# Gate and up weights converted from DRAM to DRAM, casts and copies moved between tiles, and the last output projections reordered

## What is computed

```python
xn = _layernorm(x)
# attention branch, H = 1024, chunk 32, 4 heads (DK 128, DV 256)
delta = shifted(xn) - xn
x5  = tanh((xn + delta * x0_mu) @ x0_w.T)            # 5 low-rank mixes
mix = einsum(x5, x2_w) + x_bias                      # r_mu, w_mu, k_mu, v_mu, g_mu
r, k, v, g = ((xn + delta * mu) @ W.T for r, k, v, g)
w   = -exp(tanh((xn + delta * w_mu) @ w_w1.T) @ w_w2.T + w_b2)
o   = chunk_rwkv6(r, k, v, w, bonus)                 # state carried over chunks
s   = (group_norm(o) * silu(g)) @ o_w.T
# feed-forward branch, int32 weights / 127, hidden size 3072
f   = (silu(xn @ wg.T) * (xn @ wu.T)) @ wd.T
out = x + s * silu(f)
```

## Time and profile before

| | |
|---|---|
| median of 3 runs | 1784.55 us |
| the profiled execution, its own time | 1784.01 us |
| its slowest core's span (core 3) | 1782.5 us |
| spans of the eight cores | 1767.7 to 1782.5 us |
| PE busy | 1674.2 us, 94% |
| DVE busy | 1089.5 us, 61% |
| ACT busy | 477.1 us, 27% |
| DMA packets of POOL's queue | 66.76 MB written, 23.8% of 16 engines |
| DMA packets of ACT's and SP's queues | 153.11 and 81.90 MB, 25.7% and 12.9% |
| casts of gate/up units | 72, median 11.2 us from issue to landing |
| loads of kept gate/up units | 120, median 3.9 us |
| keeps of gate/up units | 24, median 8.3 us |

### The profile page before, as it was taken

One profiled execution on the slowest core, in us unless ns is written; L12 is line 12 of the kernel. 1 busy time (PEld: TensorE's weight loads), 2 busy tenths in 40 slices (PEclk: granted clock), 3 DMA queues, 4 the chain that ended last, 5 costly groups with the idle time before them and its releaser, 6 DMA issues.

```text
span 1782.5 us, 26448 instructions; the slowest of 8 cores (1767.7 to 1782.5 us)
## 1 busy us (share of the span) xinstructions
PE 1674.2 (94%) x9248; PEld 779.5 (44%) x9248; DVE 1089.5 (61%) x1847; ACT 477.1 (27%) x802; POOL 164.1 (9%) x354
## 2 busy tenths in 40 slices
PE   4989939899899999999999999999999999999997
PEld 2333414344444445444544445444454445444453
DVE  5465616475765657648576567656576485764755
ACT  0133301143211432114321343114321143211411
POOL 2211300111101011000100002000010001100000
PEclk9999959999999999999999999999999999999999
DMA  8999996996669953877355344453636353464231
GB/s 160 173 168 211 214 226 157 181 181 162 195 166 221 205 188 131 257 191 226 130 176 202 130 176 168 151 188 113 210 119 225 130 176 132 138 228 142 95 109 58
DMA packets 77649, 303.46 MB, mean 170 GB/s; under 512 B 10511, under 2 KB 15056, under 8 KB 70864
## 3 DMA queue, kind: packets, MB, share of 16 engines
q10 hardware_dynamic: 31680, 153.11, 25.7%
q0 software_dynamic: 19680, 66.76, 23.8%
q1 hardware_dynamic: 26160, 81.90, 12.9%
HBM read 320.25 MB, written 44.04 MB: 204 GB/s over the span
## 4 chain that ended last, share of the span: by engine, by line
PE 80%; DMA 12%; DVE 3%; issue 2%; DVEq 1%; ACT 1%; SPq 1%; POOL 0%; ACTq 0%; POOLq 0%
PE PB L1209 16%; PE PB L1214 16%; PE PB L1334 8%; PE PB L1323 7%; PE PB L1490 6%; PE PB L1467 6%; PE PB L1362 6%; DMA sb_gu<-w_gu 4%; DMA sb_wd<-kept_wd 3%; PE PB L1429 3%; PE PB L1413 3%; DMA sb_wd<-w_fd 2%; DMA kept_gu<-sb_gu 2%; PE PB L1242 1%; DMA sb_xin<-x 1%
## 5 line engine op out<-in xcount | busy, mean ns | idle before, releaser
L1209 PE MATMUL PB<-sb_xnT,sb_gu 128*128 128x512 bf16 x1536 | 369.5, 384 | 22.2 <-DMA sb_gu<-w_gu 15.2
L1214 PE MATMUL PB<-sb_xnT,sb_gu 128*128 128x512 bf16 x1536 | 364.8, 380 | 0.0
L905 DVE SCALAR_TENSOR_TENSOR sb_xin<-PB,sb_xb,sb_dT 128x512 bf16<-128x512 f32 x320 | 218.1, 744 | 177.3 <-PE PB L1242 177.0
L686 ACT ACTIVATE sb_scr<-PB 128x512 bf16<-128x512 f32 x192 | 113.7, 597 | 576.3 <-PE PB L1214 534.5
L1209 PEld LDWEIGHTS PB<-sb_xnT,sb_gu 128*128 128x128 bf16 x1536 | 141.3, 98 | 211.9 <-issue 64.8
L1214 PEld LDWEIGHTS PB<-sb_xnT,sb_gu 128*128 128x128 bf16 x1536 | 151.0, 98 | 183.8 <-issue 4.4
L837 DVE SCALAR_TENSOR_TENSOR sb_hall<-PB,sb_scr 128x512 bf16<-128x512 f32 x192 | 130.5, 684 | 131.1 <-ACT sb_scr L686 131.1
L1323 PE MATMUL PB<-sb_wd,sb_hall 128*128 128x512 bf16 x768 | 180.1, 383 | 23.5 <-DMA sb_wd<-w_fd 21.2
L1334 PE MATMUL PB<-sb_wd,sb_hall 128*128 128x512 bf16 x768 | 179.8, 383 | 18.5 <-DMA sb_wd<-kept_wd 10.5
L695 ACT ACTIVATE sb_wc<-PB 128x512 bf16<-128x512 f32 x64 | 38.2, 597 | 326.1 <-PE PB L1334 326.1
L1334 PEld LDWEIGHTS PB<-sb_wd,sb_hall 128*128 128x128 bf16 x768 | 74.2, 98 | 109.7 <-issue 25.2
(11 more groups left out here) (149 smaller groups left out, 1705.6 us busy)
## 6 DMA issues: line engine op xcount, KB each, us to landing
sb_gu<-kept_gu ACTq DMA_DIRECT2D x120, 512.0 KB, 3.9
sb_ring<-kept_ring ACTq DMA_DIRECT2D x44, 1024.0 KB, 6.6
sb_wd<-kept_wd ACTq DMA_DIRECT2D x56, 768.0 KB, 7.5
sb_gu<-w_gu POOLq DMA_DIRECT2D x72, 512.0 KB, 11.2
sb_xin<-x SPq DMA_DIRECT2D x48, 512.0 KB, 7.6
kept_gu<-sb_gu SPq DMA_DIRECT2D x24, 512.0 KB, 8.3
sb_ring<-w_g POOLq DMA_DIRECT2D x16, 512.0 KB, 11.9
kept_ring<-sb_ring SPq DMA_DIRECT2D x8, 1024.0 KB, 15.2
```

The lines of the kernel that those rows point to most:

```text
L686: e.activation(out=sb_scr[:, p, :], in_=GB[p][:], func=AF.Silu, bias=0.0, scale=INV127).then_inc(a_silu, 1)
L905: e.scalar_tensor_tensor(out=sb_xin[:, p, c, :], in0=PM[j][:], scalar=sb_xb[:, n, c:c + 1], in1=sb_dT[:, c, :], op0=ALU.add, op1=ALU.mult) ...
L1209: e.matmul(GB[p][:], sb_gu[:, sl, 0, c, :], sb_xnT[:, c, :], start=(c == 0), stop=(c == NC - 1))
L1214: i = e.matmul(UB[p][:], sb_gu[:, sl, 1, c, :], sb_xnT[:, c, :], start=(c == 0), stop=(c == NC - 1))
```

## The change

Six things change together.

1. The gate/up units are no longer kept from SBUF. `convert(b)` issues, on POOL's queue, DMAs that read the 4-byte unit in DRAM and write bf16 to `kept_gu` in DRAM, in four batches: 6 units behind t = 2 and 4 units behind t = 3 of tile 1, 7 and 7 at the same places of tile 2. Batch 0 is cast for the last time in tile 1, the others in tile 2 (before: tiles 1, 2 and 3, eight units each). That makes 66 casts to SBUF, 24 conversions and 126 loads. `cast_gu` no longer waits for a keep, and `load_gu` waits for the whole batch of its unit.
2. The ring weights r and k are cast in tiles 0 to 2 (before 0 and 1), g in 0 to 2 (before 0 to 3), o in 0 and 1 (before 0 only). The casts of the next tile's r and k go behind t = 2 in tile 0 and behind t = 0 after it; the keeps move with them.
3. `load_wd` of the next tile's half 0 goes from the end of the tile to behind units 19 to 22 of the tile that uses it.
4. `load_res` of t = 2 and 3 waits for u = 4 of the down projection to be done, not for the last scores. In SP's order the first store goes ahead of the keeps of half 1.
5. At the start, POOL issues the first two unit casts behind the statistics of the first rows, and VectorE clears the state before any input is there.
6. In tile 7 `out_proj(2)` and the transposes for t = 3 go between the two halves of u = 7, `out_proj(2)` into other PSUM banks, and the last rows are added and stored in two halves.

The core of the diff:

```diff
-LAST_CAST_GU = [1 + (h + h // 3) % 3 for h in range(NHC)]
-LAST_CAST_RING = [1, 1, 2, 2, 3, 3, 0, 0]
+CONVERT = [[11, 13, 15, 17, 19, 21], [0, 1, 2, 3],
+           [4, 5, 6, 7, 8, 9, 10], [12, 14, 16, 18, 20, 22, 23]]
+BATCH = {hc: b for b, hcs in enumerate(CONVERT) for hc in hcs}
+LAST_CAST_GU = [1 if BATCH[h] == 0 else 2 for h in range(NHC)]
+LAST_CAST_RING = [2, 2, 2, 2, 2, 2, 1, 1]
...
+    def out_banks(it, t):
+        return PB[2:4] if it == LAST and t == 2 else P_o
...
         def load_res(it, t):
...
-                e.wait_ge(t_mt, 4 * (it + 1))
+                e.wait_ge(t_D, 8 * it + 5)
...
         def cast_gu(it, hc):
...
                 e.wait_ge(t_gu, n - NGU + 1)
-                kept = gu_counts(*divmod(n - NGU, NHC))[2]
-                if kept:
-                    e.wait_ge(k_gu[sl], 16 * kept)
...
+        def convert(b):
+            for hc in CONVERT[b]:
+                e.dma_start(kept_gu[hc], wdr["w_gu"][hc],
+                            max_dma_last_dim=8192).then_inc(k_gu[b], 16)
...
+                if t == (0 if it else 2) and nxt:
+                    for j in (0, 1):
+                        cast_ring(it + 1, j, 0)
+                        cast_ring(it + 1, j, 1)
+                if t >= 2 and it in (1, 2):
+                    convert(2 * it + t - 4)
...
         def load_gu(it, hc):
...
-            kept = gu_counts(it, hc)[2]
-            if it <= LAST_CAST + 1:
-                e.wait_ge(k_gu[sl], 16 * kept)
+            b = BATCH[hc]
+            e.wait_ge(k_gu[b], 16 * len(CONVERT[b]))
             e.dma_start(sb_gu[:, sl], kept_gu[hc]).then_inc(l_gu[sl], 16)
...
             for hc in range(19, 24):
                 silu_gu(it, hc)
+                if hc < 23:
+                    load_wd(it, 0, hc - 19)
...
                 down_first(it, 2 * t + 1)
+                if t == 3 and not nxt:
+                    out_proj(it, 2)
+                    og_transpose(it, 3)
                 down_second(it, 2 * t + 1)
```

## The result

The changed kernel took 1816.6 us, the median of four runs (1809.41 to 1818.3), beside 1786.5 (1784.49 to 1791.99) for the kernel before in the same session. The ratio is 1.0156, with a 95% interval of 1.0118 to 1.0194. The forecast was 1761, with a range that ended at 1785. The direction itself was wrong.

The account below looks back on a forecast made before the run. PE was taken to set the time from tile 2 on, with losses in tile 0, tile 1, small waits and the tail: 1784.0 - 22 - 3.5 - 8 - 5.1 - 1 + 13.5 + 3 = 1760.9, forecast 1761, range 1743 to 1785.

Parts of the forecast that it names:

- Part 1: Tile 0: half 1's eight down-weight casts end at 236 to 238 us, not 259; gain 22 us (17 to 25).
- Rival E: Tile 0: x loads and tile 1's casts still stand ahead of the eight casts; gain 8 for 22, total 1775; chance 0.08.
- Part 2: First stretch of tile 1: no cast waits for a keep and half 0's load is gone; gain 3.5 us (0 to 10.1).
- Part 6, tile 2: Ten conversions at 4.1 us each delay tile 2's casts, so PE waits 15.5 us for unit 9; cost 13.5 us.
- Part 6, tile 3: ACT, waiting for conversion batches at unit loads, brings a copy 2 us late and an evacuation 1 late; cost 3 us.
- Rival D: Conversions take 6 us, order on POOL and ACT decides: tile 2 costs 32, tile 3 26, total 1802; chance 0.08.
- Part 3: Residual loads no longer delay half 1's loads: 1.8 us lost per tile before; gain 8 us over tiles 3 to 7.
- Part 4: Tail: 3.2 us of waits for two ACT copies go, last addition and store get shorter; gain 5.1 us (3.2 to 6).
- Part 5: Start: x lands some 3 us sooner and 2 us of clears leave the chain; gain 1 us (-1 to 4).

Follow-up runs that it names:

- e11: Kernel before with one order changed: in tile 0 alone the casts of r and k stand behind the eight casts of half 1; ratio 0.9885 to before.
- e6: Changed kernel without conversions (units kept from SBUF), with the old ring table and loads of x ahead of o's keeps; 1760.6 us, ratio 0.982 to before.
- e4: Kernel before plus useless DMAs on POOL's queue, four each: conversions in tile 5, plain copies in tile 6, casts in tile 7; one execution of 1796.0 us.
- e8: Changed kernel with a semaphore for each conversion, so a load waits for its own unit and not the whole batch; ratio 1.0128 to before.
- e2: Kernel before with the 24 conversions in place of unit keeps, with their unit table and batch waits, nothing else of the change; ratio 1.0369 to before.
- e9: Kernel before plus twelve useless DMAs at once on POOL's queue: conversions in tile 4, plain copies in tile 6; one execution of 1831.4 us.

## Why the prediction was wrong

By its own steps:

- **Part 1, tile 0: right.** -22 predicted, -23.4 measured; u = 4's last cast at 238.1, predicted 236 to 238. e11 shows that the casts' order makes 18 of it. Rival E had no share.
- **Part 2, tile 1: the first step that failed.** -3.5 and "at u = 4 of tile 1 keeps leave and casts of r and k come: 0" were taken; tile 1 lost 14.5. The recast of r and k and the keeps of o, r and k were priced, within the 10.1 us of DMA time, but booked against the room of 431 to 512 us alone, for tile 2. The second cast of o, 13.4 us for a load of 5.5, stands in no term at all: it is issued from 388 us on, ahead of that stretch. From 110 to 170 us behind the end of tile 0 the share went from 0.65 to 1.03, and the keeps of o, x and the down weights stand in it. e6 gives all of it back by the table. The casts and keeps that the table adds to tile 1 are 27 us of DMA time, of which 18 were lost, although 21 us of that stretch had been free.
- **Part 6, tile 2: right in kind, half in size.** +13.5 predicted, +29.8 measured. On core 4 the waits for casts are 20.0, where 15.5 was worked out: the price taken, 4.1, is that of a short burst (3.72 to 4.15 in e4), and these bursts have 4.7, 6 us more for ten. Against the tile's start the first cast landed 11 us later than in the sum: at 531.8 with the start at 508.6, for 534.0 with the start at 522.3. The 6 are half of that; the other half no run splits. The order of events was as the sum had it. Two things were missing. The copy for tile 2's last projection, put at 2 late and into tile 3, came 10.2 late, because ACT stands at the whole batch (e8 takes 9.3 us away with the unit waits). And the waits cost more than their length: 9.7 of core 4's 39.9 us stand in neither, and in 8.6 of them PE is busy with the same matmuls at a lower clock.
- **Part 6, tile 3: wrong.** +3 predicted, +19.1 measured. It was worked out from what waits for a batch (with unit waits, e8, tile 3 is no shorter), not from loads that wait for nothing and share the engines with one. That `sb_gu<-kept_gu` takes 26.11 us was in no rival. Rival D had the nearest total (1802, slower, 0.08) and sizes near those measured (32 and 26 for 29.8 and 19.1), by luck: it wanted 6 us a conversion, where 3.7 to 4.9 were measured, and in tile 3 ACT's wait for a batch, whose removal in e8 gives that tile nothing.
- **Part 3: right in kind, too large.** PE's waits for half 1 in tiles 4 to 6 on core 4 (950 to 1600 us), answering, are now

```profile
PE PB L1352 <- DMA sb_wd<-kept_wd: 1.7, 3, 0.9
```

  for 5.0 before on the same core. The tiles gained 1.1 each (629.1 to 625.8 over three), predicted 1.8. The 3.3 gained are the 3.3 of waiting that went: here a wait cost its own length and no slower matmuls around it.
- **Part 4: right.** The chain of the tail, against the earlier trace rows:

```profile
1803.08 2.97 PE PB L1384 x13
...
1809.09 3.47 PE PB L1384 x16
...
1812.65 0.69 DVE sb_x L1072
...
1813.42 0.69 DVE sb_k L1077
```

  A half of u = 7 lies over each copy; from the last matmul to the span's end it is 3.9 us for 5.9. With the 3.2 of waits gone that is 5.2, for 5.1 predicted.
- **Part 5:** 1 predicted; nothing shows it. e6 has part 5 and e11 has not, and their tile 0 is 283.1 and 282.8.

What was off: tile 1 by 18, tile 2 by 16, tile 3 by 16, parts 3 and 5 by about 4, less 1 in tile 0: 53 in all, in the mean of the cores. From 1761 to 1816.6 it is 55.6, since the kernel before came out at 1786.5 beside it, 2.5 above the 1784.0 of the sum. The Trainium skill, HBM Reference, Specifications (TRN2), gives about 358 GB/s for each core of a pair, from which 4.4 us a conversion was estimated. The bursts of twelve agree with that (4.1 to 4.9), the bursts of four lie below it, and the price alone would not have given the loss.

What stays open: why the conversions cost more in e2 than inside the change; and why a conversion costs more in long bursts than in short ones. That the bursts of paired cores then overlap more was the idea, and no run separates it.

## What to carry to other kernels

Price new DMA work in the stretch in which it is issued, and only against room that comes after its issue; a mean share over 60 or 80 us says little (tile 1 lost 18 us for the new table where 21 had been free). A burst on one queue took half of the engines for as long as it stood there, and an in-order queue of loads beside it handed the delay on to PE, so work that no one waits for still has to be spread, and where the engines are full spreading does not help. Where a wait at the end of a queue is the target, move first what stands ahead of it and is needed later: here four casts moved gave 18 us in tile 0.

## What the runs showed of the hardware

- In bursts of four, a DMA that reads 4-byte numbers and writes bf16 took 2.75 to 3.26 us of the 16 engines per 512 KB written to SBUF and 3.72 to 4.15 to DRAM; a plain copy from DRAM to DRAM took 1.6 to 2.4 (e4, eight cores). Casting adds more than writing to DRAM does.
- With conversions queued, ACT's queue moved 3.11 MB in 35.9% of 35 us, 247 GB/s of its own engine time, for 313 in the same part of the tile before (5.82 MB in 53.2%). It has a third less of the engines, and moves a fifth less in what it has (e9, core 4).
- Twelve plain copies at once, 2.5 to 2.9 us each over the 50 us from the burst's start, still made the following tile 9 us longer (e9).
